# Delta-rule attention and experts on one core: the last token of each chunk read from the state behind it, and three tiles a block sent to the experts

## What is computed

```python
def step(S, inp):                       # per sequence and head, S is 8x8
    k_t, q_t, v_t, beta_t, a_t = inp
    S = S * a_t[..., None, None]
    kv_mem = jnp.einsum('bhd,bhde->bhe', k_t, S)
    delta = (v_t - kv_mem) * beta_t
    S = S + k_t[..., :, None] * delta[..., None, :]
    y_t = jnp.einsum('bhd,bhde->bhe', q_t, S)
    return (S, y_t)
...
ctx = _rmsnorm(ys, norm_w) * jax.nn.silu(gate)
x1 = _layernorm(x + ctx @ Wo.T + bo)
e = argmax(x1 @ router_w.T)             # of 8 experts
out = _layernorm(x1 + (silu(x1 @ gate_w[e].T) * (x1 @ up_w[e].T)) @ down_w[e].T)
```

## Time and profile before

| | |
|---|---|
| median of 3 runs | 808.16 us (805.93 to 808.61) |
| span of the profiled execution | 808.6 us |
| PE matmul busy | 689.3 us, 85% |
| DVE busy | 630.6 us, 78% |
| POOL busy | 642.0 us, 79% |
| ACT busy | 414.5 us, 51% |
| mean granted TensorE clock | 0.912 |

### The profile page before, as it was taken

The page is one execution under the profiler, slowest core; times in us unless marked ns, Lnnn a source line. Parts: engine busy times, 40 slices in busy tenths (PEclk is TensorE's granted clock), DMA queues, the critical chain, the costliest instruction groups (busy, mean ns, idle before and its releaser), DMA issues.

```text
span 808.6 us, 13837 instructions
## 1 busy us (share of the span) xinstructions
PE 689.3 (85%) x3545; PEld 516.8 (64%) x3545; DVE 630.6 (78%) x1697; ACT 414.5 (51%) x1281; POOL 642.0 (79%) x789
## 2 busy tenths in 40 slices
PE   8679788998999989899899995977775769999991
PEld 3436465566756657566575564756665769999890
DVE  3899999999999999999999999899611524666430
ACT  6635555457564575645656455232231245666561
POOL 2989999899999999999999999987537334444574
PEclk9989999999999999999999997878677789999996
DMA  6823234333343332443333422064433355767630
GB/s 171 206 75 94 82 103 115 87 81 98 94 116 102 82 97 80 110 121 82 89 88 110 109 69 82 17 199 143 158 109 116 119 170 184 244 231 235 224 109 8
DMA packets 135918, 97.27 MB, mean 120 GB/s; under 512 B 95630, under 2 KB 110225, under 8 KB 135714
## 3 DMA queue, kind: packets, MB, share of 16 engines
q1 hardware_dynamic: 130514, 87.55, 36.7%
q0 software_dynamic: 4320, 8.43, 3.2%
q10 hardware_dynamic: 1008, 0.43, 0.2%
HBM read 39.80 MB, written 31.43 MB: 88 GB/s over the span
## 4 chain that ended last, share of the span: by engine, by line
DVE 36%; PE 34%; POOL 13%; issue 5%; ACT 4%; another core or an unknown queue 4%; SPq 1%; DMA 1%; POOLq 0%; DVEq 0%; ACTq 0%
PE banks L433 10%; PE banks L689 7%; DVE banks L1852 6%; DVE upd L1840 6%; DVE banks L1826 5%; PE banks L446 5%; DVE prod L1810 4%; POOL q_prod L1290 4%; DVE banks L1836 4%; DVE mix L1830 4%; DVE upd L1821 3%; PE banks L742 2%; POOL u L1290 2%; PE banks L674 1%
## 5 line engine op out<-in xcount | busy, mean ns | idle before, releaser
L1290 POOL TENSOR_TENSOR q_prod<-s_keep,q_gam 128x512 f32<-128x512 f32 x128 | 139.9, 1097 | 12.8 <-ACT s_keep L1000 11.8
L742 PE MATMUL banks<-q_prod,ident 128*128 128x256 f32 x496 | 119.6, 397 | 23.8 <-POOL q_prod L1290 23.6
L1000 ACT ACTIVATE s_keep<-banks 128x128 f32<-128x128 f32 x128 | 49.8, 389 | 158.5 <-DVE upd L1840 158.5
L742 PEld LDWEIGHTS banks<-q_prod,ident 128*128 128x128 f32 x496 | 96.1, 199 | 49.0 <-POOL q_prod L1290 35.7
L433 PE MATMUL banks<-xs_t,w_tile 128*128 128x128 f32 x852 | 114.1, 284 | 13.0 <-ACT xs_t L463 5.2
L542 POOL DMA_INDIRECT out<-rows_out,xs x71 | 70.0, 986 | 59.7 <-ACT rows_out L523 53.2
L433 PEld LDWEIGHTS banks<-xs_t,w_tile 128*128 128x128 f32 x852 | 106.0, 199 | 16.4 <-issue 9.3
L1852 DVE TENSOR_REDUCE banks<-upd 128x128 f32<-128x640 f32 x127 | 105.1, 827 | 7.6 <-DVE upd L1840 0.5
L577 DVE TENSOR_TENSOR hid<-banks,silu 128x384 f32<-128x384 f32 x71 | 39.6, 558 | 89.6 <-PE banks L433 36.3
L689 PE MATMUL banks<-kkqk,ident 128*128 128x320 f32 (+2 forms) x272 | 88.6, 488 | 9.9 <-ACT y_rms L1028 5.3
L1826 DVE TENSOR_REDUCE banks<-prod 128x64 f32<-128x576 f32 x128 | 93.7, 732 | 0.0
(11 more groups left out here) (219 smaller groups left out, 1459.9 us busy)
## 6 DMA issues: line engine op xcount, KB each, us to landing
w_tile<-gate_up_we SPq DMA_DIRECT2D x71, 352.0 KB
xs<-x_sorted SPq DMA_DIRECT2D x71, 64.5 KB
x_ct<-in_x_ct SPq DMA_DIRECT2D x16, 256.0 KB, 3.0
k_dram<-kq_s SPq DMA_DIRECT2D x16, 256.0 KB, 3.0
q_dram<-kq_s SPq DMA_DIRECT2D x16, 256.0 KB, 3.7
out<-v_s SPq DMA_DIRECT2D x16, 256.0 KB, 2.7
out<-beta SPq DMA_DIRECT2D x16, 256.0 KB, 2.6
k_h<-k_dram SPq DMA_DIRECT2D x16, 256.0 KB
```

The costliest lines, as they stand in the source:

```text
L742: i = mm(out, ident[:, :], q_prod[m][:, :, d, :], start=(m == 0 and d == 0), stop=(d == DH - 1), skip_group_check=True)
L1290: b.step(label, win, lambda: tt(out, x, y, op))
```

## The change

It does two things.

1. **The last token of a chunk.** Since y_t is read behind its own update, the output of a chunk's fourth token is its raw q times the state with which the next chunk begins. So `q_gam` of a chunk now holds the last token's q of the chunk before in slot 0, copied by ACT without a decay (`q_raw`, and `q_next` across a block's edge), and q with decays for its own first three tokens in slots 1 to 3. `q_prod` keeps its size. The lags inside a chunk are for three tokens: `y_prod` and POOL's qk products have three parts (384, 256 and 128 elements) for four, `kkqk` 256 columns for 320. The last token of a block comes from the next block's first q_prod, by a small sum on DVE, `y_next`, which writes it to `y_ps` before ACT squares. It stands behind the update of chunk 2, in block 15 behind that of chunk 1. In the tail DVE makes the last state too, and `y_ends` and `y_next`. Outputs now lie in the order of the tokens, so the gate's projection is written without a permutation (`project_gate`). `y_sums` moves behind the lag sums and k norms on PE and to another bank, `y_square` and `y_root` move later on ACT, and the parts of `y_n` from chunks 3 to 5 to chunks 4 to 7 (in block 15 they stay).
2. **Sorts.** `SORTED` becomes three tiles a block from block 4 on: 33 sent before block 15, 13 in it, 18 in the tail. There six stand ahead of the context product and four behind it, now those of block 13, ahead of `ln_r`.

```diff
@@ -152,7 +153,7 @@
-q_prod = two_a("q_prod", [P, 4, DH, DH * 2 * C])
+q_prod = two_a("q_prod", [P, DH, DH * 2, T // 2])
...
@@ -629,8 +630,7 @@
-SORTED = {w: max(w - 4, 0) for w in range(-2, NW - 2)}
-SORTED.update({NW - 2: 10, NW - 1: 13})
+SORTED = {w: max(3 * (w - 4), 0) for w in range(-2, NW)}
...
@@ -672,6 +672,10 @@
+    def project_gate(bank, win=a):
+        b.step("g", win, lambda: mm(bank, w_proj[:, 3, :], x_ct[win % 2][:, :], start=True, stop=True))
...
@@ -733,26 +737,30 @@
+    def y_slots(win):
+        return y_ps[win % 2].rearrange("p (n t) -> p n t", t=T)
-        out = y_ps[win % 2].rearrange("p (n c) -> p c n", c=NCH)[:, 4 * m:4 * m + 4, :]
+        out = y_slots(win)[:, :, 0:T // 2 - 1] if m == 0 else y_slots(win)[:, :, T // 2 - 1:T - 1]
-                i = mm(out, ident[:, :], q_prod[m][:, :, d, :], start=(m == 0 and d == 0),
+                i = mm(out, ident[:, :], q_prod[m][:, d, :, 1 - m:], start=(m == 0 and d == 0),
-        y = y_ps[p % 2].rearrange("p (n m) -> p n m", m=C * NCH)
+        y = y_ps[p % 2].rearrange("p (n c j) -> p n j c", c=NCH, j=C)
-            for d in range(C):
-                size = (C - d) * NCH
-                i = mm(y[:, :, d * NCH:], ident[:, :], y_prod[:, at:at + DH * 2 * size], start=False, stop=True,
+            for d in range(C - 1):
+                size = (C - 1 - d) * NCH
+                i = mm(y[:, :, d:C - 1, :], ident[:, :], y_prod[:, at:at + DH * 2 * size], start=False, stop=True,
...
@@ -921,10 +931,11 @@
+        b.wait(act, "y_r0", w - 2)
-        project("g", 3, pre_ps[:, 1, :])
+        project_gate(pre_ps[:, 1, :])
-            b.wait(dve, "qkd3", a - 2)
+            b.wait(dve, "qkd2", a - 2)
...
@@ -940,35 +951,33 @@
-        b.wait(pool, "y_prod3", p)
+        b.wait(pool, "y_prod2", p)
-            b.wait(pool, "qk3", 0)
-            lag_sums("kkqk", 0, pre_ps[:, 2, :], 96, 256)
+            b.wait(pool, "qk2", 0)
+            lag_sums("kkqk", 0, pre_ps[:, 2, :], 96, 192)
-    if b.post:
-        b.wait(dve, "qkd3", n - 1)
-        b.wait(act, "v_s", a)
-        y_sums(p, pre_ps[:, 2, 0:2 * T])
-        b.wait(act, "y_r0", p)
-        b.wait(pool, "qk3", n)
-        b.wait(dve, "qkd3", n - 1)
-        lag_sums("kkqk", n, pre_ps[:, 2, :], 0, 320)
+        b.wait(pool, "qk2", n)
+        b.wait(dve, "qkd2", n - 1)
+        lag_sums("kkqk", n, pre_ps[:, 2, :], 0, 256)
+    if b.post:
+        b.wait(act, "kq_s", min(a, NW - 1))
+        y_sums(p, pre_ps[:, 1, 0:2 * T])
...
@@ -992,16 +1001,13 @@
-        if g < NW * NCH - 1:
-            b.wait_chunks(s_upd, 2 * g + 2)
-        else:
-            b.wait_chunks(s_delta, g + 1)
+        b.wait_chunks(s_upd, 2 * g + 2)
-        to = d_keep[win % 2][:, :, :, c] if win < NW - 1 else d_last[:, :, :, c]
-        b.wait(pool, "y_prod3", win - 2)
-        b.step(f"d_keep{c}", win, lambda: A(to, bank[:, P:P + 64].rearrange("p (n j) -> p n j", j=C), ACT.Copy))
+        to = d_keep[win % 2][:, :, 0:C - 1, c] if win < NW - 1 else d_last[:, :, 0:C - 1, c]
+        b.wait(pool, "y_prod2", win - 2)
+        b.step(f"d_keep{c}", win, lambda: A(to, bank[:, P:P + 64].rearrange("p (n j) -> p n j", j=C)[:, :, 0:C - 1], ACT.Copy))
...
@@ -1017,12 +1023,13 @@
+        b.wait(dve, "y_next", p)
-        sums = pre_ps[:, 2, 0:2 * T] if p < NW - 1 else post_ps[:, 0:2 * T]
+        sums = pre_ps[:, 1, 0:2 * T] if p < NW - 2 else pre_ps[:, 2, 0:2 * T] if p == NW - 2 else post_ps[:, 0:2 * T]
...
@@ -1056,8 +1063,17 @@
-        b.step("q_sq", win, lambda: A(kkqk[:, :, 256:320] if win else y_sq[:, :, :],
+        b.step("q_sq", win, lambda: A(kkqk[:, :, 192:256] if win else y_sq[:, :, :],
+    def q_ends(win):
+        b.wait(pool, "q_prod7", win - 2)
+        b.step("q_raw", win, lambda: A(q_gam[win % 2][:, 1:NCH, :, :, 0].rearrange("p c d b -> p d b c"),
+                                       q_h[win % 2][:, :, :, C - 1, 0:NCH - 1], ACT.Copy))
+        to = q_gam[(win + 1) % 2][:, 0, :, :, 0] if win < NW - 1 else q_end[:, :, :]
+        b.wait(pool, "q_prod0", win - 1)
+        b.step("q_next", win, lambda: A(to, q_h[win % 2][:, :, :, C - 1, NCH - 1], ACT.Copy))
...
@@ -1255,17 +1270,20 @@
-        y_root()
+        y_square()
+    if b.post:
+        y_root()
+        q_ends(n)
...
@@ -1295,19 +1313,22 @@
+        if c == 0:
+            b.wait(dve, "y_next", win - 2)
+            b.wait(act, "q_next", win - 1)
+        if c == 1:
+            b.wait(act, "q_raw", win)
-        mul(f"q_prod{c}", win, q_prod[c // 4][:, c % 4, :, :].rearrange("p d (e b j) -> p d e b j", e=DH, b=2),
-            s, q)
+        at = c * C % (T // 2)
+        mul(f"q_prod{c}", win, q_prod[c // 4][:, :, :, at:at + C].rearrange("p d (e b) j -> p d e b j", b=2), s, q)
-        mul("ctx", o, ctx_t[:, :].rearrange("p (b c j) -> p b j c", b=NB, j=C),
-            y_ch[:, :].rearrange("p (b j c) -> p b j c", b=NB, j=C),
-            gate[o % 5][:, :].rearrange("p (b j c) -> p b j c", b=NB, j=C))
+        mul("ctx", o, ctx_t[:, :], y_ch[:, :], gate[o % 5][:, :])
...
@@ -1323,11 +1344,11 @@
-        for d in range(C):
-            size = (C - d) * NCH
+        for d in range(C - 1):
+            size = (C - 1 - d) * NCH
-                qh[:, :, :, d:C, :].rearrange("p d b j c -> p d b (j c)"),
-                kh[:, :, :, 0:C - d, :].rearrange("p d b j c -> p d b (j c)"))
+                qh[:, :, :, d:C - 1, :].rearrange("p d b j c -> p d b (j c)"),
+                kh[:, :, :, 0:C - 1 - d, :].rearrange("p d b j c -> p d b (j c)"))
...
@@ -1339,14 +1360,14 @@
-        b.wait(dve, "qkd3", p)
+        b.wait(dve, "qkd2", p)
-        for d in range(C):
-            size = (C - d) * NCH
+        for d in range(C - 1):
+            size = (C - 1 - d) * NCH
-                d_keep[p % 2][:, :, 0:C - d, :].rearrange("p (e b) j c -> p e b (j c)", b=2),
+                d_keep[p % 2][:, :, 0:C - 1 - d, :].rearrange("p (e b) j c -> p e b (j c)", b=2),
...
@@ -1416,13 +1438,13 @@
-        sort_to(w0, w0 + 10)
+        sort_to(w0, (NW - 3) * TW)
-        sort_to(w0 + 10, w0 + 14)
+        sort_to((NW - 3) * TW, (NW - 2) * TW)
-        for win in range((w0 + 14) // TW, NW):
-            sort_to(max(w0 + 14, win * TW), (win + 1) * TW)
+        sort_to((NW - 2) * TW, (NW - 1) * TW)
+        sort_to((NW - 1) * TW, NW * TW)
...
@@ -1534,9 +1557,29 @@
-    def qkd_part(d):
-        at = lag_at[d]
-        b.step(f"qkd{d}", n, lambda: v.tensor_tensor(lag(qd, at + 64, d), lag(ps, at + 160, d), by[d - 1], ALU.mult))
+    def q_lag(tile, at, d):
+        return tile[:, at:at + 2 * (C - 1 - d) * NCH].rearrange("p (b j c) -> p b j c", b=2, c=NCH)
+    def qkd_part(d, win=n):
+        to, at = qkd[win % 2], (0, 48, 80)[d]
+        al_w, dk_w = a_h[win % 2], decays[win % 2]
+        if d == 0:
+            b.step("qkd0", win, lambda: v.tensor_copy(to[:, 0:48], ps[:, 96:144]))
+        else:
+            over = al_w[:, :, 1:C - 1, :] if d == 1 else dk_w[:, :, 4:5, :]
+            b.step(f"qkd{d}", win, lambda: v.tensor_tensor(q_lag(to, at, d), q_lag(ps, 96 + at, d), over, ALU.mult))
+    def q_norm_part(win=n):
+        b.step("q_norm", win, lambda: v.tensor_scalar(
+            q_norm[win % 3][:, :].rearrange("p (b c j) -> p b j c", b=2, j=C),
+            ps[:, 192:256].rearrange("p (b j c) -> p b j c", b=2, j=C), DH * DH * RMS_EPS, None, ALU.mult))
+    def y_next_part():
+        b.wait(pool, "q_prod0", w)
+        b.wait(pe, "y", p)
+        b.step("y_next", p, lambda: v.tensor_reduce(
+            y_ps[p % 2].rearrange("p (n t) -> p n t", t=T)[:, :, T - 1],
+            q_prod[0][:, :, :, 0].rearrange("p d n -> p n d"), AX, ALU.add))
...
@@ -1687,31 +1724,34 @@
-        if b.post and c == 3 and 3 <= k:
-            if k == 3:
-                b.wait(act, "y_r1", p)
-            y_n_part(k - 3)
+        if b.post and c == 2 and k == 3:
+            y_next_part()
-            y_n_part(k - 1)
+            if k == 3:
+                b.wait(act, "y_r1", p)
+            y_n_part(k - 3)
-            y_n_part(k + 4)
+            y_n_part(k + 2)
-            b.step("q_norm", n, lambda: v.tensor_scalar(q_norm[n % 3][:, :], ps[:, 256:320], DH * DH * RMS_EPS, None,
-                                                        ALU.mult))
-        if b.pre and c == 6 and k == 0:
-            b.step("qkd0", n, lambda: v.tensor_copy(qd[:, 0:64], ps[:, 96:160]))
-        if b.pre and c == 6 and 1 <= k < 4:
+            q_norm_part()
+        if b.pre and c == 6 and k < 3:
+        if b.post and c == 6 and k == 3:
+            y_n_part(6)
+        if b.post and c == 7 and k == 1:
+            y_n_part(7)
+        if c == 1 and k == 3:
+            y_next_part()
...
@@ -1744,18 +1784,29 @@
-            e.wait_ge(s_delta, NN)
+            e.wait_ge(s_state, NN)
+        b.wait(act, "q_next", NW - 1)
+        ends = mix[:, :, :, :].rearrange("p n i j -> p n (i j)")[:, :, 0:DH]
+        b.step("y_ends", p, lambda: v.tensor_tensor(
+            ends.rearrange("p (e b) d -> p e b d", b=2),
```

(27 more changed lines are left out.)

32 lines of the change are left out of this document (13 added, 19 removed).

## The result

| | before | after |
|---|---|---|
| median | 807.04 us (803.31 to 808.61, 4 runs) | 794.47 us (792.72 to 797.25, 4 runs) |
| span of the profiled execution | 808.6 us | 790.9 us |
| mean granted TensorE clock | 0.912 | 0.910 |

The ratio is 0.984, 95% interval 0.981 to 0.987: 12.6 us less by the medians, 17.7 by the two profiled executions (that of before is at the long end of its runs, that of after is the shortest of its own). The forecast was 797.0.

What follows compares the result with a forecast made beforehand. DVE's recurrence was taken as the bound, POOL just beneath, then PE's tile pace. Running total: -7.3, -2.5 after block 15, -6.2 in the tail, +0.1 at ln_r, then -11.7 for the hole: 808.6 - 11.6 = 797.0 us, range 789 to 810.

Steps and rivals of the forecast that it cites:

- The kkd wait: Blocks 3 to 10 and 14: DVE's kkd no longer waits for PE's lag sums, -7.3 us at block 15's start.
- my bound of 1.1: Upper bound in us, over all blocks, for DVE's new small step y_next; taken as 0.
- POOL's play: Slack on POOL, taken to absorb k_h landing 0.3 us late in the next block, at no cost.
- q_prod's time: POOL's q_prod, output now in runs of four, keeps 1097 ns; bounds 1097 and 1271, up to +1.4 us a block.
- The late norm: Norm, root and y_n later in each block: fits with nearly no margin; rival that it holds the recurrence, chance 0.11.
- Block 15: Late y of block 13 makes the recurrence wait 5.6 us; y_n(14) ends 4.8 later, leaving -2.5 at y(14)'s load.
- Tail: Behind block 15: y_deltas shorter by 1.8 us, root 1.9 earlier; -6.2 in all at the places of block 13.
- ln_r behind four sorts: POOL's ln_r waits for block 13's four sorts, 608.0 for 605.77; a step back to +0.1 at PE's turn.
- The hole: PE from turn to last count: 15.4 us for 27.1 once the row of sixteen sorts is broken up, -11.7.
- my bound of 14: Lower bound in us for PE's turn to last count, its work laid end to end; upper bound 19.
- Rival (a): The hole stays because it follows PE's and ACT's code, not the sorts: 811.3 us, slower; chance 0.13.
- the root's -1.9: ACT's root of block 15 starts 1.9 us earlier with six sorts left there for ten.

Runs made afterwards that it cites:

- c2: The kernel after, unchanged, on the second set's chip without the hole: 789.4 us, ratio 1.012 to the kernel before.
- f3: f2 with SP storing k and loading q and k ahead of y's store and load in each block: 790.2 us, ratio 0.977.
- f4: f2 with the old sending of sorts (one a block, sixteen in a row, ln_r ahead of them): 815.9 us, ratio 1.008.
- e3: The kernel after with POOL's ln_r of block 15 ahead of the four sorts of block 13: 781.8 us, ratio 1.003.
- f2: f1 with POOL's ln_r of block 15 ahead of the four sorts of block 13: 792.0 us, ratio 0.979.
- g2: f4 with a POOL multiplication of 128x384 unneeded elements behind each of the sixteen sorts: 809.7 us, ratio 0.998.
- c1: The kernel before, unchanged, profiled on the second set's chip without the hole: 780.1 us.
- g1: f3 without f1's order; in block 15 y_next at the end of chunk 2, ACT's keeps and root earlier: 797.0 us, ratio 0.981.
- f1: The kernel after with block 15 reordered: block 14's y work ahead of block 13's context product and projection: 796.0 us, ratio 0.983.

## Why the prediction was right, and where it wasn't

*The kkd wait* (-7.3 at block 15's start): it went wholly, blocks 4 to 14 stand at 33.5 and block 3 at 33.9. Measured -5.2 (530.76): two terms were mis-sized and two missed. y_next costs 0.09 us in each chunk 2 (4.25 for 4.17), 1.2 in all and above my bound of 1.1, where I took 0; its gap wasn't wide enough. And k_h and q_h, which I let vanish in POOL's play, cost 0.8 us in block 2 (34.30) and in c2 2.6 in block 3 (36.51 for the 33.90 that f3 leaves). Missed were 0.4 more in block 3, and 0.4 less in block 0: -7.3 + 1.2 + 0.8 + 0.4 - 0.4 = -5.3.

*q_prod's time*: 1100 ns for 1097, as taken. *The late norm*: it fits with the margin that I gave, nearly none; f4 shows it fail by 1.6 us in some blocks.

*Block 15*: the stall was 5.0 for 5.6. The load of y_ch(14) was -0.2 for -2.5, since less had been won before, and from store to load it took 3.1 us for 2.5.

*Tail*: y_deltas took 2.87 for 4.41, -1.5 for -1.8. The root -7.3 for -6.2: from the end of y_deltas to the root it was 6.7 us in before and 2.9 in after, so the row of ten had cost 3.8, and I had read only the 1.9 behind PE's sums. PE and y_square were late beside it too; the chain of before has 5.69 us released by nothing known there (from 584.94). Places of block 13 -8.5 for -6.2.

*ln_r behind four sorts*: the step back came as forecast, and e3 puts it at some 7 us, f2 at 4 by the medians. ln_r was at 605.70 for 608.0, the turn at 607.99 for 610.3, as the place had come earlier.

*The hole*: 11.5 us from turn to last count, for 15.4 and below my bound of 14, so -15.6 for -11.7; I had laid a low clock and waits on PE end to end that cost less. This was the term that carried the result, and its cause was argued, not shown. Now: f2 and f4 differ in POOL's sorts alone, on one chip, and the hole comes with the row; g2 puts pauses between the same sorts and the hole goes. Rival (a), that it follows the code, falls. DMA: Bandwidth & Descriptors of the Trainium skill, section Queues, rings and completion order, by which the queues take turns, doesn't foresee it. Nor is the load of instruction blocks late, as far as the DMA view shows it. On the instruction queue q8, which I take for PE's, one block moves between 606.5 and 607.0 and the next between 634.5 and 635.0 in the kernel before, between 602.5 and 603.0 and between 612.5 and 613.0 in the same kernel without hole. These are nearly the same places in PE's code (within 4 us of its counts of blocks 13 and 15); none lies within the hole, and PE doesn't pause at any of the four. There the trace agrees with Runtime: NRT & Kernel Launch, section Instruction fetch mechanics, by which crossing a block is mostly hidden. What PE waits for is open.

*The sum.* By the two traces it is -2.2 at the turn (forecast +0.1) and -15.6 in the hole, 17.8 in all, and the end comes 17.7 earlier. That the medians differ by 12.6, beside a forecast of 11.6, is in part luck: both main terms were mis-sized on the same side, and the two profiled executions lie at opposite ends of their kernels' runs. The 808.6 that I started from is a span too, and every run's time is 1.8 us above its span.

*What the argument missed* is that the hole isn't a trait of the kernel alone. I took one profile for the kernel. Without the hole two of my terms have nothing to win (-11.7 and the root's -1.9), and the rest came to +10 in c2 against c1: -2.6 at block 15's start, +6.1 from there to the places of block 13 (late y, and PE's norm sums at a granted clock of 0.50, 3.7 us for 2.0), +7.6 at ln_r, -1.0 behind it. The forecast of 797 was right for a chip where the hole is, as the one behind the profile and the result.

## What to carry to other kernels

A gap that the profile puts down to nothing known should be seen on a second chip before a change is valued by it: here the same edit gives -1.6% on one and +1.2% on the other. Break up long rows of indirect DMAs. Where the hole exists, ACT's root started 0.03 to 0.04 us after PE's sums behind six sorts (in all five kernels) and 2.3 to 5.4 us after them behind ten, and sixteen cost 15.5 us. Short groups weren't wholly free there: beside groups of four PE paused 2.4 us in f2, f3 and g1, and ACT began its squares 1.9 and 2.9 us late in f4 and g2. But don't break rows up by putting them ahead of a step on the way to the end: ln_r before four sorts was worth 4 to 7 us. Taking out one wait on the bound engine (f1, g1) gave nothing: in g1 the next wait on the same late queue took its place, in f1 the moved step set off big loads beside the store that mattered.

## What the hardware showed that I hadn't expected

The kernel before takes 779.1 and 779.8 us on two chips and 807.0, 808.5 and 811.7 in the other sets, with a mean granted clock of 0.93 against 0.91 in the profiles of c1 and of the result. The sorts themselves don't differ. The DMA view, first of the kernel before in the result's profile (616 to 628), then on the chip without hole (the same stretch of time, also within its row of sorts):
```profile
q0 software_dynamic: 320, 0.66, 16.5%
```
```profile
q0 software_dynamic: 310, 0.62, 16.2%
```
Nearly as many packets take the same share of the DMA engines, POOL keeps the same beat of 1.26 us, and beside it PE starves on the one and not on the other. In the tile stage, too, pauses stand on the chips with the hole and none on the others, whatever the kernel: 146.1 to 150.6 us for 140.3 to 142.0. What sets the chips apart, I can't tell from these traces.
